# A sort step's lower half copied to PSUM by ScalarE before VectorE takes minimum and maximum

## The reference

```python
def _L1_gnn_ref(x, A_indices, A_values, A_shape, W, bias, gamma, beta):
    h = jnp.einsum('nd,df->nf', x, W)
    row, col = (A_indices[0], A_indices[1])
    gathered = A_values[:, None] * h[col]
    agg = jax.ops.segment_sum(gathered, row, num_segments=A_shape)
    h = agg + bias
    ...
```

```python
    src = jnp.concatenate([edge_index[0], loops])
    dst = jnp.concatenate([edge_index[1], loops])
    ...
    agg = jax.ops.segment_sum(msg, dst, num_segments=M)
```

## Time and profile before

| | us |
|---|---|
| median of 3 runs | 9306.64 |
| lowest, highest | 9304.74, 9342.89 |
| the profiled execution's own time | 9387.91 |
| its span, first to last instruction | 9386.1 |
| first aggregation, about | 220 to 2565 |
| second aggregation, about | 4156 to 6591 |

### The profile page before, as it was taken

One profiled execution on the slowest core, in us unless ns is written; L12 is line 12 of the kernel. 1 busy time (PEld: TensorE's weight loads), 2 busy tenths in 40 slices (PEclk: granted clock), 3 DMA queues, 4 the chain that ended last, 5 costly groups with the idle time before them and its releaser, 6 DMA issues. The chain is left out here.

```text
span 9386.1 us, 89224 instructions
## 1 busy us (share of the span) xinstructions
PE 5874.7 (63%) x19881; PEld 3964.3 (42%) x19881; DVE 4494.3 (48%) x8790; ACT 3781.8 (40%) x9693; POOL 4973.1 (53%) x4762
## 2 busy tenths in 40 slices
PE   5455555555569999655555555555647677676755
PEld 4333333333356666333443333333624444444444
DVE  4444555545569999564544444444711111111125
ACT  5555555555552222444554554555401111111113
POOL 4666666666542222546666666666454544454532
PEclk8666667777659999876776676676568878787878
DMA  5333333333321111542332222232321111111126
GB/s 147 99 99 100 98 100 101 95 90 89 100 97 41 50 54 41 142 150 87 89 89 84 86 83 83 84 89 81 130 56 43 41 41 41 42 42 42 44 74 253
DMA packets 500454, 797.42 MB, mean 85 GB/s; under 512 B 123070, under 2 KB 365355, under 8 KB 499851
## 3 DMA queue, kind: packets, MB, share of 16 engines
q0 software_dynamic: 200256, 453.47, 18.0%
q1 hardware_dynamic: 299696, 338.23, 11.2%
HBM read 595.60 MB, written 197.30 MB: 84 GB/s over the span
## 5 line engine op out<-in xcount | busy, mean ns | idle before, releaser
L1017 PE MATMUL part<-rows,spread 128*128 x6656 | 2441.4, 523 | 2142.5 <-issue 1124.7
L1017 PEld LDWEIGHTS part<-rows,spread 128*128 128x128 f32 x6656 | 1624.7, 261 | 2905.8 <-issue 2631.6
L974 DVE TENSOR_TENSOR agg<-agg,part 128x257 f32 (+1 forms) x3328 | 1405.6, 422 | 2401.1 <-issue 866.3
L957 POOL DMA_INDIRECT rows<-h,row x1563 | 1555.7, 995 | 876.9 <-issue 439.9
L957 POOL DMA_INDIRECT rows<-f,row x1563 | 1555.2, 995 | 767.3 <-issue 456.8
L1041 ACT ACTIVATE spread<-iota,place 128x128 f32<-128x128 f32 x3328 | 1020.2, 392 | 2186.2 <-PE part L1017 1057.9
L1921 POOL DMA_INDIRECT rows<-gat,src x1122 | 1062.0, 947 | 1097.4 <-DVEq L2108 764.5
L1996 PE MATMUL y_ps<-agg,hid 128*128 128x256 f32 x3136 | 888.0, 423 | 658.4 <-issue 653.1
L1996 PEld LDWEIGHTS y_ps<-agg,hid 128*128 128x128 f32 x3136 | 661.1, 212 | 906.0 <-issue 821.1
L1047 ACT ACTIVATE spread<-spread,weight 128x128 f32<-128x128 f32 x3328 | 1021.2, 391 | 14.5 <-ACT spread L1043 0.9
L2126 DVE TENSOR_TENSOR y_all<-y_ps,b 128x512 f32<-128x512 f32 x196 | 135.5, 692 | 1792.1 <-DMA h<-res 1046.2
(11 more groups left out here) (393 smaller groups left out, 6035.2 us busy)
## 6 DMA issues: line engine op xcount, KB each, us to landing
expert_rows<-y_all SPq DMA_DIRECT2D x196, 256.0 KB
made<-expert_rows SPq DMA_DIRECT2D x49, 1024.0 KB
x<-x SPq DMA_DIRECT2D x42, 896.0 KB
rows<-f,row POOLq DMA_INDIRECT x1563
rows<-h,row POOLq DMA_INDIRECT x1563
rows<-gat,src POOLq DMA_INDIRECT x1122
xbuf<-zero SPq DMA_DIRECT2D x128, 128.0 KB
x<-xbuf SPq DMA_DIRECT2D x32, 512.0 KB
```

What stands on the lines that cost most here:

```text
L957: pool.indirect_dma_start(out=rows[:, u, 0:D], out_offset=None, in_=table, in_offset=bass.IndirectOffsetOnAxis(ap=q.row[:, i:i + 1], axis= ...
L974: nc.vector.tensor_tensor(sum_t, sum_t, part[:, p % NB, 0:WIDE], ALU.add).then_inc(added, 1)
L1017: nc.tensor.matmul(part[:, p % NB, 0:WIDE], spread[:, p % (2 * BANKS), :], row_p, start=True, stop=True).then_inc(multiplied, 1)
```

## The change

For swaps of the second sort before the merge, ScalarE copies the lower halves of all pairs from the key buffer to `lift`, one PSUM bank of 128x512 in fp32, and counts `held`. VectorE waits for `held` ahead of the minimum; minimum and maximum then read `lift` (PSUM) as first operand and the key buffer (SBUF) as second. `lift` takes a bank, so `NB` goes from 7 to 6 in the second aggregation. The 18 swaps of the merge are as before, and so is the first aggregation.

```diff
+    def lifted(self, i):
+        return not self.weighted and i < self.joint
...
-            link(nc.vector.tensor_tensor(b[:, :, 0, :], a[:, :, 0, :], a[:, :, 1, :], ALU.min))
-            link(nc.vector.tensor_tensor(b[:, :, 1, :], a[:, :, 0, :], a[:, :, 1, :], ALU.max))
+            low = a[:, :, 0, :]
+            if w.lifted(i):
+                low = w.lift[:, 0:n // 2].rearrange("p (m d) -> p m d", d=by)
+                dve.wait_ge(w.held, w.swaps[i] + 1)
+            link(nc.vector.tensor_tensor(b[:, :, 0, :], low, a[:, :, 1, :], ALU.min))
+            link(nc.vector.tensor_tensor(b[:, :, 1, :], low, a[:, :, 1, :], ALU.max))
...
-            pay = w.pay[:, :].rearrange("p (m h d) -> p m h d", h=2, d=by)
-            copy(w.spare[:, :].rearrange("p (m d) -> p m d", d=by), pay[:, :, 0, :]).then_inc(w.held, 1)
+            if w.weighted:
+                pay = w.pay[:, :].rearrange("p (m h d) -> p m h d", h=2, d=by)
+                copy(w.spare[:, :].rearrange("p (m d) -> p m d", d=by), pay[:, :, 0, :]).then_inc(w.held, 1)
+            elif w.lifted(i):
+                n = w.width(i)
+                key = w.key[w.swaps[i] % 2][:, 0:n].rearrange("p (m h d) -> p m h d", h=2, d=by)
+                copy(w.lift[:, 0:n // 2].rearrange("p (m d) -> p m d", d=by), key[:, :, 0, :]).then_inc(w.held, 1)
...
-        NB = BANKS if last_i is None else BANKS - 1
+        NB = BANKS if last_i is None else BANKS - 2
+        if not w.weighted:
+            w.lift = s.ps("lift", [P, 512])
...
-                def hold_payload(g):
-                    if w.weighted:
-                        sort_holds(act, lambda out, src: nc.scalar.activation(out, src, ACT.Copy), w, share(g), share(g + 1))
+                def hold_halves(g):
+                    sort_holds(act, lambda out, src: nc.scalar.activation(out, src, ACT.Copy), w, share(g), share(g + 1))
```

More of the change, by code:

```diff
@@ L284, in __init__ @@
     def __init__(self, s, free, weighted, joined=False):
+        self.lift = None
         self.free, self.n, self.weighted = free, (2 if joined else 1) << free, weighted
@@ L1056, in _ @@
                         spread_weights(g + 1)
-                    hold_payload(g)
+                    hold_halves(g)
 def route_first(nc, k, sums, x1, dest, send, fetch, scale):
```

## The result

The changed kernel takes 9330.54 us in the median (12 runs, 9312.25 to 9366.13) against 9305.65 (12 runs, 9289.29 to 9342.89): 1.0031 of before, 95% interval 1.0018 to 1.0043. The forecast was 9282, faster by 0.27%. The time lies outside the forecast's own 9260 to 9300, inside the range widened for the rivals (9224 to 9345), and the sign is the other one.

What follows compares the result with a forecast made beforehand. It took GpSimd's queue, waits included, in a loop with TensorE's freeing of the ring, to bound the second aggregation. Terms -40 + 0 + 0 + 15 = -25 us turned 9306.64 into 9282 us; own range 9260 to 9300, widened 9224 to 9345.

Steps and rivals of the forecast that it cites:

- Part one: GpSimd's gathers in the second aggregation: 153 swaps no longer stretch them, 0.38 us each, 58 us, of which 40 arrive.
- the upper bound of 72 us: Second aggregation: whole excess of 1563 gathers, mean 995 over median 949 ns, including `hot` and the merge swaps.
- the common wait of 3.1 us: GpSimd's usual wait for a freed ring group, thought tied to the last gather, so earlier gathers move the cycle forward.
- rival 1: Second aggregation: gathers stay stretched or the time won is waited away; 9307 to 9322, say 9312 us; chance 0.22.
- the sign of its forecast: GpSimd's waits for `freed` in the second aggregation stay near 407 us, at 440 (407 + 18 + 15).
- the turns: 16 places where TensorE waits for VectorE to drain; gain of 48 swaps lost there, 18 us.
- Parts two and three: VectorE's swaps reading `lift` and waiting on `held`, and ScalarE's 153 copies of 0.68 us: cost 0 each.
- Part four: Second aggregation with six banks: TensorE fewer pairs ahead, 15 waits longer by about 1 us, 15 us cost.
- Rival 3: Sixth bank: at each of 123 ring waits GpSimd waits 1.3 us more, 160 us; +120 net, 9427 us; chance 0.15.

Runs made afterwards that it cites:

- copies unused: Changed kernel with minimum and maximum reading the key buffer for both operands, copies, `held` wait and six banks kept: 1.0011 and 1.0014 of the kernel before.

## Why the prediction was wrong

**What bounds the kernel.** The prediction took GpSimd's queue, waits included, for the bound, since the parts add up to the stretch. Work and waits of any engine add up to its stretch. The 407.4 us of waits were the sign that GpSimd was not the bound. On the quick chip, where it is, they are gone.

**Part one, the stretch.** 58 us were forecast from four samples of 0.38 us. The trace after gives 20, the same-chip pairs 13 on a slow chip and 16 to 23 on the quick one. The mechanism is right: what stood beside the swaps is gone to the last gather. The size is off by the samples. The whole trace before has 22 us beside 153 swaps, 0.14 us each. Three of the samples (4922.16, 5437.85, 5445.59) did start inside a swap, with 0.40, 0.21 and 0.40 us, but the median gather that does so has 0.08. The fourth, at 5281.34, started inside `hot`, just ahead of the swap, and the 45 us of excess in the trace that start there are more than the swaps' own. So of the upper bound of 72 us, less than a third was the swaps'.

**How much reaches the end: the step that failed.** The prediction said that the common wait of 3.1 us hangs on the last gather, so that 40 of 58 us pass through. On a slow chip next to nothing passes: 91 us of added work were met by 80 us less of waits, and 13 us of shorter gathers brought no time. On the quick chip all of it does. The reading behind the step was wrong too. From a mean of 3.3 us it took most of the 123 waits to be of the common size; 59 of them lie between 2.5 and 3.4 us, 41 are shorter, and 23 are longer, with 171 of the 407.4 us. This is rival 1 in its second half, "the time won is waited away", which had 0.22. The prediction gave its reason (the waits were seven times what was to be won) and set it aside for the common wait. Rival 1's time, 9307 to 9322, was still too short by 8 us or more.

That the waits came to 441.1 us, where the prediction had 440 as the sign of its forecast, is luck. That figure was added to the waits of a profile with other surroundings, and meant 18 us lost at the turns and 15 for the bank. On one chip, copies with seven banks against the changed kernel, the waits rise by 54 us (361.0 to 414.5), not by 33.

**Parts two and three** held: 685 and 692 ns, idle time ahead 0.6 us in 153, copies of 590 ns (0.68 was forecast), no cost on either kind of chip (1.0014 against 1.0016; 0.9993 and 1.0003 with the copies alone).

**Part four**, 15 us for the bank: 12 and 10 us over the kernel before on the slow chips, nothing on the quick one. Rival 3 has the right place and the wrong price; a cost of its size, 121 us, is there only with four banks. One reason against it was misread: between the end of the swap in rows 7 and GpSimd's wait lie 9 us of gathers (4923.42 to 4932.29), not 13.

**What stays open.** The sum by parts on a slow chip is 10 to 15 us for the bank, and 22 to 30 were measured. The rest, 12 to 15 us or 0.13 to 0.15%, stands on one chip between the changed kernel and the two with six banks that read SBUF (9327.71 against 9315.30 and 9312.18). The intervals of these ratios still touch; drawing again from the 11 runs of each, the changed kernel stands 2 to 25 us above the one that does not read its copies. The waits agree: 29 us more there, and 460.8 us on the chip of 9378 us against 430.0 and 420.1 us for six banks and for copies unused on the one of 9387. It is not the copies and not the wait on `held`.
## What to carry to other kernels

Before a saving on an engine is counted, ask whether that engine waits for something downstream in the same stretch: if its waits are larger than the saving, a pause put in its place tells in one run how much of its time is on the path. A handful of samples picked because they are long does not give a mean: count the excess over all instances, by what each one starts in. And a ratio of 0.3% may change its sign with the chip, if the issuing engine bounds the kernel on one and the loop that gives it its buffers back on another.

## What the runs showed of the hardware

The same kernel takes 7775 us on one chip and 9306 to 9387 on others, and nine tenths of the difference lie in the three stretches with GpSimd gathers (315, 371 and 750 of 1611 us); most of the rest is in the last stretch (386 against 235 us). The experts' stretch between the aggregations is alike, by windows first of the slow, then of the quick chip (six banks there):

```profile
core 0: us, PE busy (x) PEld busy (x) DVE busy (x) ACT busy (x) POOL busy (x), PEclk, DMA share, GB/s
...
2565.00:4150.00 1585.00, 1348.80 (x5364) 898.02 (x5364) 1284.94 (x1715) 539.23 (x1198) 510.48 (x329) 0.88 0.28 84
4150.00:6591.00 2441.00, 1329.38 (x4511) 929.76 (x4511) 1165.01 (x2287) 1257.22 (x3536) 1555.74 (x1563) 0.70 0.30 85
```
```profile
2250.00:3830.00 1580.00, 1349.07 (x5370) 899.28 (x5370) 1290.39 (x1737) 538.87 (x1199) 509.97 (x329) 0.88 0.28 86
3830.00:5900.00 2070.00, 1169.41 (x4545) 922.68 (x4546) 1174.08 (x2284) 1261.94 (x3540) 1567.17 (x1564) 0.79 0.35 102
```

1585 against 1580 us there, 2441 against 2070 in the second aggregation, with nearly the same busy time on VectorE, ScalarE and GpSimd. TensorE differs: it is busy 1329 us against 1169, at a granted clock of 0.70 against 0.79, while in the experts' stretch both are alike (0.88). Whether the lower clock there is a cause of the longer stretch or follows from TensorE's idle time no run here separates. On the slow chips VectorE's idle time ahead of its additions is for a large part unexplained ("remote" 453.3 us and "issue" 261.6); on the quick chip it waits for TensorE and for its own last addition:

```profile
DVE agg L989 <- PE part L1032: 702.7, 951, 4.9
DVE agg L989 <- DVE agg L989: 157.1, 707, 0.7
```

One more thing differs. Of SyncE's 3588 semaphore instructions 464 to 570 last over 0.5 us in each of the twelve profiles that ran like the slow chips, and one in each of the eight from quick chips; in the profile before all but one of the 570 lie in the two aggregations. On VectorE it is 299 of 4323 in the profile before, and 2 in each of the eight. So semaphores seem to be slow on the slow chips while gathers run; what delays them no run here shows.

A gather is stretched where it starts while an instruction with two SBUF operands is already running, and not where it was there first. In the profile before, the 118 gathers that start inside `hot` take 1.33 us in the mean. The 109 that start during an addition and run on beside `hot` take 0.95, none of them over 0.964. ScalarE's copy of 128x512 takes 590 ns into PSUM (the changed kernel) and 627 ns into the key buffer in SBUF (the chip of 9306 us).
